# First attention of a four-layer kernel: one exp of half the scores, scaled and squared, in place of two exps with a shift between

## The chip, the cores and the metric

The kernel runs on one core of a Trainium2 chip. The metric is the device time of one execution in microseconds; times inside the profiled execution are counted from its first instruction.

## The reference

The whole kernel computes four layers over x of shape (32, 16, 16, 64): a shifted-window attention, a convolution with computed taps (involution), a linear attention with a mixture of experts, and a second linear attention with a routed mixture. The change touches the first:

```
xw  = windows of the rolled, group-normed x        # 128 windows of 64 tokens, 8 heads of 8
attn = (qn @ kn^T) * scale + bias + mask           # qn, kn: rows of length 1
attn = softmax(attn)
out  = attn @ v, then @ Wo.T + bo, rolled back, and added to x
```

A softmax may be taken of shifted scores, since the quotient stays the same: exp(s - c) / sum exp(s - c).

## The kernel before

**Tiling.** The activations lie channel by token: 128 partitions (64 channels of two halves of the batch) by 4096 columns, eight chunks of 512 (`NCH`). The attention works in 64 window pairs (`PAIRS`), two to a unit: 32 units (`UNITS`), four to a chunk (`PER`). A unit has two halves b = 2u and 2u+1, each a tile of 128 by 512 scores in a PSUM bank of its own (banks 0 to 3 in turns of two units).

**A unit before.** POOL spreads the unit's queries over the heads (`stage_queries`, L692). PE writes bias and mask (L1939, two matmuls) and then the products of queries and keys (L1945, 16 small matmuls) into the two banks. ACT takes exp of half the scores of each bank into a bf16 tile (`exp_half`, L1576). PE sums these over the keys with a matrix of ones into bank 4 (`sum_halves`, L1955), so that every row holds the sum. DVE reads the sum's bits as an integer, which is nearly its logarithm, and makes of it the level to take away, minus twice that logarithm (L914), and adds the level to the scores (L919), both in `shift_down`. ACT takes exp of the shifted scores (`exp_scores`, L1584). PE multiplies with the values (L1966) and sums for the denominator (L1969), both in `weigh`, into bank 5 or 6. ACT inverts the denominator by Ln and Exp (`invert_sums`, L1590 and L1592), DVE multiplies (`divide_unit`, L924). Once per chunk PE projects (`project_out`, L1981), DVE adds the result to the image in nine pieces (`add_images`, L934) and takes the statistics of the next norm (`image_stats`, L309 and L313), and ACT adds a bias to the image (`add_bias`, L1595).

**Order.** Each engine has its own list, written out by hand as a loop over k, and the engines meet at counted semaphores: `when("l0_summed", n)` is the wait until step l0_summed has been done n times. In iteration k PE does the first sum of unit k-1, the scores of unit k, the second sum of unit k-1, the weighing of unit k-2 and, in one of four, a projection. The scores of unit k wait until both halves of unit k-2 are shifted:

```
            def scores(u):
                pe.wait_ge(*when("l0_staged", u + 1))
                if u >= 2:
                    pe.wait_ge(*when("l0_shifted", 2 * (u - 1)))
```

There is one sum bank, so a sum waits until DVE has read the one before. ACT alternates the exp of half the scores of unit k with the exp of the shifted scores of unit k-1.

Elsewhere in the kernel stand L1027 (a product of two SBUF tiles on DVE), L741, L713, L750 and L767 (subtractions and a product on POOL) and L1216 (a cast on DVE), which are quoted below.

Of the kernel before, what the change touches and what calls it, by code (L numbers as in the profile page):

```python
# [5 lines left out]
F32, F16, BF16 = mybir.dt.float32, mybir.dt.float16, mybir.dt.bfloat16  # L6
# [21 lines left out]
LEVEL = -2.0 * float(np.log(2.0)) / 2.0 ** 23, 254.0 * float(np.log(2.0))  # L28
# [118 lines left out]
def network(nc, xw_d, xi_d, mats_d, vecs_d, feats_d, cw1_d, wmask_d, taps_d, wexp_d, wo0_d,  # L147
            w1l2_d, w2l2_d, w1l3_d, w3l3_d, w2l3_d, out_d, slots_d, results_d):
    with ExitStack() as ctx:
# [98 lines left out]
        SC = [stage[:, 1024 + s * 512:1536 + s * 512] for s in range(2)]  # L248
        PX = [stage[:, 2048 + s * 512:2560 + s * 512] for s in range(4)]
# [6 lines left out]
        EH = [spare[:, 512 + 256 * s:768 + 256 * s].bitcast(BF16) for s in range(2)]  # L256
        LV = [spare[:, 1024 + 512 * s:1536 + 512 * s] for s in range(2)]
# [50 lines left out]
        def gn_image(dve, t, src, b):  # L308
            nc.vector.bn_stats(stats[:, b, :], src[:, b, :]).then_inc(S(t + "_stats"), 1)  # L309
# [331 lines left out]
        def _(pool):  # L641
# [56 lines left out]
            pool.wait_ge(*when("hmask", 2))  # L698
            for u in range(UNITS):
                stage_queries(u)  # L700
# [135 lines left out]
        def _(dve):  # L836
# [74 lines left out]
            def shift_down(b):  # L911
                u, g = b // 2, b % 2
                dve.wait_ge(*when("l0_summed", b + 1))
                nc.vector.tensor_scalar(LV[b % 2], bank[4][:, :].bitcast(I32), LEVEL[0], LEVEL[1],  # L914
                                        ALU.mult, ALU.add).then_inc(S("l0_level"), 1)
                dve.wait_ge(*when("l0_level", b + 1))
                if b >= 2:
                    dve.wait_ge(*when("l0_exp", b - 1))
                nc.vector.tensor_tensor(SC[b % 2], bank[2 * (u % 2) + g][:, :], LV[b % 2], ALU.add) \  # L919
                    .then_inc(S("l0_shifted"), 1)  # L920

            def divide_unit(u):
                dve.wait_ge(*when("l0_rsum", u + 1))
# [3 lines left out]
            def add_images(c):  # L927
                dve.wait_ge(*when("xi_biased", c + 1))
                dve.wait_ge(*when("l0_wo", c + 1))
                yw = bank[7][:, :].rearrange("p (b w i j) -> p b w i j", w=NWIN, i=WS, j=WS)  # L930
                for wy, iy, r, nr in runs:
                    for wx, ix, q, nq in runs:
                        xv = Xi[:, 2 * c:2 * c + 2, r:r + nr, q:q + nq]
                        nc.vector.tensor_tensor(xv, xv, yw[:, :, 2 * wy + wx, iy:iy + nr, ix:ix + nq], ALU.add)                             .then_inc(S("x1_ready"), 1)  # L934

            def image_stats(c):
                dve.wait_ge(*when("x1_ready", 9 * (c + 1)))
                for b in (2 * c, 2 * c + 1):
                    gn_image(dve, "g1", X3, b)
                for b in (2 * c, 2 * c + 1):  # L940
                    gn_total(dve, "g1", b)
# [4 lines left out]
            for k in range(1, UNITS + PER + 1):  # L946
                if k <= UNITS:
                    shift_down(2 * k - 2)
                if 3 <= k < UNITS + 3:
                    divide_unit(k - 3)  # L950
                if k <= UNITS:
                    shift_down(2 * k - 1)
                if k % PER == 3 and k >= 7:
                    add_images(k // PER - 1)
                if k % PER == 0 and k >= 8:
                    image_stats(k // PER - 2)
# [589 lines left out]
        def _(act):  # L1546
# [24 lines left out]
            def exp_half(b):  # L1571
                u, g = b // 2, b % 2
                act.wait_ge(*when("l0_scores", u + 1))
                if b >= 2:
                    act.wait_ge(*when("l0_summed", b - 1))
                nc.scalar.activation(EH[b % 2], bank[2 * (u % 2) + g][:, :], ACT.Exp, scale=0.5) \  # L1576
                    .then_inc(S("l0_half"), 1)

            def exp_scores(b):
                u = b // 2  # L1580
                act.wait_ge(*when("l0_shifted", b + 1))
                if u >= 2:
                    act.wait_ge(*when("l0_pv", u - 1))
                nc.scalar.activation(PX[b % 4], SC[b % 2], ACT.Exp).then_inc(S("l0_exp"), 1)  # L1584

            def invert_sums(u):
                act.wait_ge(*when("l0_pv", u + 1))
                if u >= 2:
                    act.wait_ge(*when("l0_out", u - 1))
                nc.scalar.activation(RS[u % 2], bank[5 + u % 2][:, 256:512], ACT.Ln).then_inc(S("l0_lnsum"), 1)  # L1590
                act.wait_ge(*when("l0_lnsum", u + 1))
                nc.scalar.activation(RS[u % 2], RS[u % 2], ACT.Exp, scale=-1.0).then_inc(S("l0_rsum"), 1)  # L1592
# [13 lines left out]
            for k in range(UNITS + 2):  # L1606
                for g in range(2):
                    if k < UNITS:
                        exp_half(2 * k + g)
                    if 1 <= k <= UNITS:  # L1610
                        exp_scores(2 * k - 2 + g)
                if k >= 2:
                    invert_sums(k - 2)
                if k % PER == 1 and k < UNITS:
                    add_bias(k // PER)
# [264 lines left out]
        def _(pe):  # L1880
# [52 lines left out]
            def scores(u):  # L1933
                pe.wait_ge(*when("l0_staged", u + 1))
                if u >= 2:
                    pe.wait_ge(*when("l0_shifted", 2 * (u - 1)))
# [14 lines left out]
            def sum_halves(b):  # L1951
                pe.wait_ge(*when("l0_half", b + 1))
                if b >= 1:
                    pe.wait_ge(*when("l0_level", b))
                nc.tensor.matmul(bank[4][:, :], sum16, EH[b % 2], start=True, stop=True).then_inc(S("l0_summed"), 1)  # L1955

            def weigh(u):
# [4 lines left out]
                parts = [PX[(2 * u + g // 2) % 4].rearrange("p (j x n) -> p j x n", j=2, x=2)[:, :, g % 2, :]  # L1962
# [723 lines left out]
```

## Time and profile before

| what | value |
|---|---|
| time, three runs | median 1014.98 us (1014.89 to 1015.75) |
| profiled execution | 1015.97 us |
| its span, first to last instruction | 1014.0 us |
| mean granted TensorE clock | 0.938 of full |
| first attention, first scores to last addition | about 72 to 217 us |
| busy over the span | PE 84%, DVE 82%, ACT 69%, POOL 60% |

PE is TensorE, DVE VectorE, ACT ScalarE, POOL GpSimd, PEld TensorE's weight load. A duration is that of the instruction as recorded; instructions of one engine overlap a little, so the work of an engine is better read from the distance between two starts. The idle time behind a row in brackets is that ahead of the instruction, with the line that ended it.

### The profile page before, as it was taken

The numbers are of one execution on the slowest core, as the hardware profiler recorded it, in microseconds if no ns is written. First come the engines' busy times: TensorE is split into PE (matmuls) and PEld (weight loads), VectorE is DVE, ScalarE is ACT, GpSimd is POOL, SyncE is SP. The second block draws the span as 40 slices with busy tenths as digits, with TensorE's granted clock in tenths as the row PEclk, the third lists the DMA queues.
The fourth block names the chain that finished last, engine by engine and source line by source line (L and its number), as shares of the span: only waits on it lengthen the run. The fifth ranks groups of instructions, "written<-read, shape, count | busy, mean of one in ns | idle before, by whom it ended". The sixth has DMA issues, their size and how long they took to land.

```text
span 1014.0 us, 20687 instructions
## 1 busy us (share of the span) xinstructions
PE 855.2 (84%) x6419; PEld 478.1 (47%) x6440; DVE 830.1 (82%) x1720; ACT 697.0 (69%) x1318; POOL 604.0 (60%) x645
## 2 busy tenths in 40 slices
PE   4958888859999998788888987589999999999960
PEld 3433333424445763344355544255555556555640
DVE  7987888878866856687768888589999999999986
ACT  1867777736447556555777664288889999999966
POOL 1952222214787654277504777777777788888880
PEclk9978999979999999599999999599999999999985
DMA  6000000020003210000300000211111111111107
GB/s 246 1 2 2 2 2 2 2 79 0 1 1 114 70 44 0 1 2 1 100 1 14 27 26 26 61 56 47 39 45 41 33 34 35 33 35 36 36 21 250
DMA packets 25807, 39.64 MB, mean 39 GB/s; under 512 B 6436, under 2 KB 14632, under 8 KB 25448
## 3 DMA queue, kind: packets, MB, share of 16 engines
q1 hardware_dynamic: 16616, 28.93, 9.0%
q0 software_dynamic: 9088, 9.39, 2.8%
q8 instruction: 58, 0.95, 0.4%
q14 instruction: 45, 0.37, 0.1%
HBM read 24.83 MB, written 13.47 MB: 38 GB/s over the span
## 4 chain that ended last, share of the span: by engine, by line
PE 43%; DVE 23%; POOL 15%; issue 9%; ACT 7%; DMA 1%; POOLq 0%; SPq 0%; another core or an unknown queue 0%; ACTq 0%; DVEq 0%
PE bank L2495 9%; POOL results L808 6%; PE bank L2468 5%; POOL slots L785 4%; PE bank L2028 3%; DVE KSS L914 3%; POOL stage L767 3%; DVE stage L919 2%; PE bank L1945 2%; PE bank L1981 2%; DVE T L896 2%; PE bank L2045 1%; PE bank L2257 1%; PE bank L2070 1%; PE bank L1939 1%
## 5 line engine op out<-in xcount | busy, mean ns | idle before, releaser
L2495 PE MATMUL bank<-stage,big 128*128 128x512 f16 (+1 forms) x858 | 226.4, 384 | 6.9 <-issue 3.0
L808 POOL DMA_INDIRECT results<-T,small x156 | 177.7, 1139 | 44.3 <-issue 35.6
L785 POOL DMA_INDIRECT slots<-T,index x128 | 127.1, 993 | 79.3 <-DVE index L1347 41.4
L1855 ACT ACTIVATE T<-bank 128x512 f32<-128x512 f32 x234 | 139.5, 596 | 28.8 <-PE bank L2495 21.8
L1837 ACT ACTIVATE stage<-T 128x512 f16<-128x512 f32 x234 | 146.4, 626 | 3.5 <-DVE T L1494 2.1
L1494 DVE TENSOR_TENSOR T<-bank,T 128x512 f32<-128x512 f32 x195 | 133.8, 686 | 12.3 <-ACT T L1855 8.3
L1517 DVE TENSOR_TENSOR T<-T,stage 128x512 f16<-128x512 f32 x170 | 117.4, 690 | 1.2
L2495 PEld LDWEIGHTS bank<-stage,big 128*128 (+1 forms) x858 | 78.1, 101 | 59.1 <-issue 17.2
L692 POOL TENSOR_TENSOR stage<-T,small 128x512 f32<-128x512 f32 x32 | 34.2, 1068 | 99.0 <-PE bank L1945 99.0
L2468 PE MATMUL bank<-l2w,stage 128*128 (+1 forms) x936 | 90.8, 219 | 0.1
L2468 PEld LDWEIGHTS bank<-l2w,T 128*128 128x128 f16 x780 | 53.7, 98 | 69.3 <-issue 46.4
L2468 PE MATMUL bank<-l2w,T 128*128 x780 | 76.2, 220 | 9.4 <-DVE T L1517 4.9
L2468 PEld LDWEIGHTS bank<-l2w,stage 128*128 128x128 f16 (+1 forms) x936 | 63.9, 98 | 9.3 <-issue 1.3
L713 POOL TENSOR_TENSOR stage<-stage 128x512 f16<-128x512 f32 x40 | 46.1, 1160 | 33.6 <-ACT stage L1636 32.6
L914 DVE TENSOR_SCALAR KSS<-bank 128x512 f32<-128x512 int32 x64 | 43.7, 683 | 23.1 <-PE bank L1955 14.6
L767 POOL TENSOR_TENSOR stage<-stage 128x256 f16<-128x256 f32 x64 | 43.4, 695 | 30.4 <-DVE stage L1216 30.0
L1576 ACT ACTIVATE KSS<-bank 128x512 bf16<-128x512 f32 x64 | 37.6, 589 | 30.0 <-PE bank L1945 30.0
L989 DVE TENSOR_TENSOR stage<-bank,big 128x512 f32<-128x512 f32 x72 | 46.9, 687 | 8.7 <-PE bank L2045 6.4
L1700 ACT ACTIVATE stage<-bank,small 128x256 f32<-128x256 f32 x64 | 30.2, 474 | 27.5 <-PE bank L2223 27.0
L1636 ACT ACTIVATE stage<-stage 128x512 f16<-128x512 f32 x40 | 25.2, 630 | 33.6 <-DVE stage L989 33.6
L2257 PE MATMUL bank<-T,mats 128*128 128x512 f32 x64 | 37.0, 666 | 12.8 <-ACT T L1720 12.1
L1584 ACT ACTIVATE stage<-stage 128x512 f32<-128x512 f32 x64 | 40.1, 626 | 10.9 <-DVE stage L919 8.6
(395 smaller groups left out, 1970.9 us busy)
## 6 DMA issues: line engine op xcount, KB each, us to landing
stage<-slots SPq DMA_DIRECT2D x39, 130.0 KB, 2.1
stage<-in_w3l SPq DMA_DIRECT2D x8, 373.0 KB, 3.0
stage<-in_w1l SPq DMA_DIRECT2D x8, 320.0 KB, 3.0
results<-T,small POOLq DMA_INDIRECT x156
T<-in_xw SPq DMA_DIRECT2D x4, 512.0 KB, 6.1
X<-in_xi SPq DMA_DIRECT2D x1, 2048.0 KB, 13.4
slots<-T,index POOLq DMA_INDIRECT x128, 2.2
X<-results SPq DMA_DIRECT2D x8, 256.0 KB, 5.5
```

What stands on the lines that cost most here:

```text
L767: nc.gpsimd.tensor_tensor(HID_LO[n % 4], HID[n % 4], HID_HI[n % 4], ALU.subtract).then_inc(S("low3"), 1)
L785: pool.indirect_dma_start(slots_d, bass.IndirectOffsetOnAxis(ap=index[:, k, n:n + 1], axis=0), rows5[:, n * RW:(n + 1) * RW], None).then_i ...
L808: pool.indirect_dma_start(results_d, bass.IndirectOffsetOnAxis(ap=IDS[t % 4][:, i:i + 1], axis=0), Y5[t % 2][:, i, :], None).then_inc(S(f" ...
L914: nc.vector.tensor_scalar(LV[b % 2], bank[4][:, :].bitcast(I32), LEVEL[0], LEVEL[1], ALU.mult, ALU.add).then_inc(S("l0_level"), 1)
L989: nc.vector.tensor_tensor(product(k).rearrange("p (b r c) -> p b r c", r=HH, c=WW), bank[k % 6][:, :].rearrange("p (b r c) -> p b r c", r= ...
L1494: nc.vector.tensor_tensor(H5[q], bank[3 + q][:, :], S5[q], ALU.mult).then_inc(S("hid5"), 1)
L1517: nc.vector.tensor_tensor(LO5[q], H5[q], HI5[q], ALU.subtract).then_inc(S("low5"), 1)
L1837: nc.scalar.activation(HI5[q][r], H5[q][r], ACT.Copy).then_inc(S("high5"), 1)
L1855: nc.scalar.activation(S5[q][to], bank[q][r, :], ACT.Silu).then_inc(S("silu5"), 1)
L2257: nc.tensor.matmul(out, mat("mean"), T2P[c], start=True, stop=True).then_inc(S4(op), 1)
L2468: mm = nc.tensor.matmul(bank[6 + s][:, i * 128:(i + 1) * 128], H[:, i * 128:(i + 1) * 128], downs[rows_down, bass.ds(w, 2 * C)], start=(k ...
L2495: mm = nc.tensor.matmul(to[0:m, :], big16[:, bass.ds(e * UPW + o, m)], XT[s], start=(v % 2 == 0), stop=(v % 2 == 1))
```

## The change

The second exp is gone. The exp of half the scores, now kept in f32, is multiplied by the inverse of its sum and then squared, which gives the exp of the shifted scores: (exp(s/2) / sum)^2. The inverse is again made from the bits of the sum: `INVERSE` minus the integer, read as a float, is nearly the reciprocal (`invert_level`). Of a unit's two halves DVE multiplies the first (`scale_down`), POOL the second; ACT squares both (`square`). The exps of half the scores are written to eight tiles in turn (`EX`, `HELD`), in which all the rest is done in place; the sum matmul reads the high 16 bits of each f32 element as bf16, every second 16-bit element of the tile. The order changes too: ACT does the inversion of the denominators, both exps of unit k, then both squares of unit k-2; DVE does both inversions ahead of the division; POOL stages two units ahead; weighing comes one iteration later and the projection, the additions and the statistics later and in smaller parts.

```
@@ POOL
             pool.wait_ge(*when("hmask", 2))
+            stage_queries(0)
+            stage_queries(1)
             for u in range(UNITS):
-                stage_queries(u)
+                if u + 2 < UNITS:
+                    stage_queries(u + 2)
+                b = 2 * u + 1
+                pool.wait_ge(*when("l0_inverse", b + 1))
+                nc.gpsimd.tensor_tensor(EX[b % HELD], EX[b % HELD], RV[1], ALU.mult) \
+                    .then_inc(S("l0_scaled_pool"), 1)
@@ DVE
-            def shift_down(b):
-                u, g = b // 2, b % 2
+            def invert_level(b):
                 dve.wait_ge(*when("l0_summed", b + 1))
-                nc.vector.tensor_scalar(LV[b % 2], bank[4][:, :].bitcast(I32), LEVEL[0], LEVEL[1],
-                                        ALU.mult, ALU.add).then_inc(S("l0_level"), 1)
-                dve.wait_ge(*when("l0_level", b + 1))
-                if b >= 2:
-                    dve.wait_ge(*when("l0_exp", b - 1))
-                nc.vector.tensor_tensor(SC[b % 2], bank[2 * (u % 2) + g][:, :], LV[b % 2], ALU.add) \
-                    .then_inc(S("l0_shifted"), 1)
+                if b % 2 and b >= 3:
+                    dve.wait_ge(*when("l0_scaled_pool", b // 2))
+                nc.vector.tensor_scalar(RV[b % 2].bitcast(I32), bank[4][:, :].bitcast(I32), -1.0, INVERSE,
+                                        ALU.mult, ALU.add).then_inc(S("l0_inverse"), 1)
+
+            def scale_down(b):
+                dve.wait_ge(*when("l0_inverse", b + 1))
+                nc.vector.tensor_tensor(EX[b % HELD], EX[b % HELD], RV[0], ALU.mult).then_inc(S("l0_scaled"), 1)
...
-            for k in range(1, UNITS + PER + 1):
+            for k in range(1, UNITS + 2 * PER + 1):
                 if k <= UNITS:
-                    shift_down(2 * k - 2)
-                if 3 <= k < UNITS + 3:
-                    divide_unit(k - 3)
-                if k <= UNITS:
-                    shift_down(2 * k - 1)
-                if k % PER == 3 and k >= 7:
-                    add_images(k // PER - 1)
-                if k % PER == 0 and k >= 8:
-                    image_stats(k // PER - 2)
+                    invert_level(2 * k - 2)
+                    scale_down(2 * k - 2)
+                    invert_level(2 * k - 1)
+                if 4 <= k < UNITS + 4:
+                    divide_unit(k - 4)
+                c = k // PER - 2
+                if k % PER == 1 and c >= 0:
+                    add_images(c, 0)
+                if k % PER == 2 and c >= 0:
+                    add_images(c, 1)
+                if k % PER == 3 and c >= 0:
+                    image_stats(c, 0)
+                    image_stats(c, 1)
+                if k % PER == 0 and c >= 1:
+                    image_totals(c - 1)
@@ ACT
             def exp_half(b):
                 u, g = b // 2, b % 2
                 act.wait_ge(*when("l0_scores", u + 1))
-                if b >= 2:
-                    act.wait_ge(*when("l0_summed", b - 1))
-                nc.scalar.activation(EH[b % 2], bank[2 * (u % 2) + g][:, :], ACT.Exp, scale=0.5) \
+                if u >= 4:
+                    act.wait_ge(*when("l0_pv", u - 3))
+                nc.scalar.activation(EX[b % HELD], bank[2 * (u % 2) + g][:, :], ACT.Exp, scale=0.5) \
                     .then_inc(S("l0_half"), 1)
 
-            def exp_scores(b):
...
+            def square(b):
+                act.wait_ge(*when("l0_scaled_pool" if b % 2 else "l0_scaled", b // 2 + 1))
+                nc.scalar.activation(EX[b % HELD], EX[b % HELD], ACT.Square).then_inc(S("l0_exp"), 1)
...
-            for k in range(UNITS + 2):
-                for g in range(2):
-                    if k < UNITS:
-                        exp_half(2 * k + g)
-                    if 1 <= k <= UNITS:
-                        exp_scores(2 * k - 2 + g)
-                if k >= 2:
-                    invert_sums(k - 2)
+            for k in range(UNITS + 4):
+                if k >= 4:
+                    invert_sums(k - 4)
+                if k < UNITS:
+                    exp_half(2 * k)
+                    exp_half(2 * k + 1)
+                if 2 <= k < UNITS + 2:
+                    square(2 * k - 4)
+                    square(2 * k - 3)
                 if k % PER == 1 and k < UNITS:
                     add_bias(k // PER)
@@ PE
             def scores(u):
                 pe.wait_ge(*when("l0_staged", u + 1))
                 if u >= 2:
-                    pe.wait_ge(*when("l0_shifted", 2 * (u - 1)))
+                    pe.wait_ge(*when("l0_half", 2 * (u - 1)))
...
             def sum_halves(b):
                 pe.wait_ge(*when("l0_half", b + 1))
                 if b >= 1:
-                    pe.wait_ge(*when("l0_level", b))
-                nc.tensor.matmul(bank[4][:, :], sum16, EH[b % 2], start=True, stop=True).then_inc(S("l0_summed"), 1)
+                    pe.wait_ge(*when("l0_inverse", b))
+                high = EX[b % HELD].bitcast(BF16).rearrange("p (n v) -> p n v", v=2)[:, :, 1]
+                nc.tensor.matmul(bank[4][:, :], sum16, high, start=True, stop=True).then_inc(S("l0_summed"), 1)
...
-            for k in range(UNITS + 3):
+            for k in range(UNITS + 5):
...
-                if 2 <= k < UNITS + 2:
-                    weigh(k - 2)
-                if k % PER == 2 and k >= 6:
-                    project_out(k // PER - 1)
+                if 3 <= k < UNITS + 3:
+                    weigh(k - 3)
+                if k % PER == 0 and k >= 8:
+                    project_out(k // PER - 2)
```

## Rows read from the trace of the kernel before

**Rows 1.** The page's first line.
```profile
span 1014.0 us, 20687 instructions
```

**Rows 2.** Stretches: us, each engine's busy us (instructions), granted clock, DMA.
```profile
72.00:82.00 10.00, 7.78 (x43) 2.93 (x45) 3.17 (x6) 2.94 (x6) 2.08 (x2) 0.50 0.00 0
...
98.40:114.80 16.40, 14.27 (x186) 6.48 (x184) 14.00 (x34) 12.32 (x26) 4.17 (x4) 1.00 0.01 1
```

**Rows 3.** Waits from 98.4 to 196.6 us: total us, times, longest.
```profile
PE bank L1939 <- DVE stage L919: 8.8, 18, 1.0
...
ACT KSS L1576 <- PE bank L1945: 16.2, 18, 1.8
```

**Rows 4.** PE's timeline in one chunk: start, us, line, operands, count.
```profile
147.16 1.09 PE L1945 MATMUL bank<-stage,T 32*64 32x256 f32 x16
148.18 0.39 PE L1955 MATMUL bank<-KSS,rows 128*128 128x512 bf16 x1
148.50 0.64 PE L1966 MATMUL bank<-stage,big 128*32 128x128 f32 x16
148.96 0.61 PE L1969 MATMUL bank<-stage,small 128*32 128x256 f32 x8
149.51 1.98 PE L1981 MATMUL bank<-T,big 128*128 128x512 f32 x4
151.33 0.38 PE L1955 MATMUL bank<-KSS,rows 128*128 128x512 bf16 x1
151.54 0.59 PE L1939 MATMUL bank<-big,rows 128*128 128x512 f16 x2
152.07 1.09 PE L1945 MATMUL bank<-stage,T 32*64 32x256 f32 x16
```

**Rows 5.** PE's timeline at the attention's start, middle and end.
```profile
81.86 1.01 PE L1939 MATMUL bank<-big,rows 128*128 128x512 f16 x2
...
86.92 0.59 PE L1939 MATMUL bank<-big,rows 128*128 128x512 f16 x2 [0.52 <-DVE stage L919]
...
105.98 0.59 PE L1939 MATMUL bank<-big,rows 128*128 128x512 f16 x2 [0.27 <-DVE stage L919]
...
203.52 0.39 PE L1955 MATMUL bank<-KSS,rows 128*128 128x512 bf16 x1
...
212.18 1.22 PE L1981 MATMUL bank<-T,big 128*128 128x512 f32 x1 [1.41 <-DVE T L924]
```

**Rows 6.** POOL's L750 and L713: ns min/median/max, first and last start, shapes.
```profile
L750 POOL TENSOR_TENSOR T<-T x8: 1035/1040/1477, 322.4 to 360.1; 128x512 f32<-128x512 f32 x8
...
L713 POOL TENSOR_TENSOR stage<-stage x40: 1155/1160/1163, 239.2 to 297.0; 128x512 f16<-128x512 f32 x40
```

**Rows 7.** Timeline of POOL and DVE, later in the kernel.
```profile
327.94 1.40 POOL L741 TENSOR_TENSOR big<-stage,big 128x640 f16<-128x640 f32 x1
328.25 1.63 DVE L1027 TENSOR_TENSOR T<-T 128x512 f32<-128x512 f32 x1
...
334.72 0.69 DVE L1027 TENSOR_TENSOR T<-T 128x512 f32<-128x512 f32 x1 [0.42 <-ACT T L1645]
```

**Rows 8.** DVE's timeline in the chunk of rows 4.
```profile
151.74 0.69 DVE L914 TENSOR_SCALAR KSS<-bank 128x512 f32<-128x512 int32 x1 [1.72 <-PE bank L1955]
152.47 0.69 DVE L919 TENSOR_TENSOR stage<-bank,KSS 128x512 f32<-128x512 f32 x1
153.08 0.41 DVE L924 TENSOR_TENSOR T<-bank,KSS 128x256 f32<-128x256 f32 x1
```

**Rows 9.** Timeline: an instruction on DVE and what it releases, twice.
```profile
161.45 0.68 DVE L914 TENSOR_SCALAR KSS<-bank 128x512 f32<-128x512 int32 x1
...
162.28 0.38 PE L1955 MATMUL bank<-KSS,rows 128*128 128x512 bf16 x1 [0.16 <-DVE KSS L914]
...
428.55 0.29 DVE L1216 CAST stage<-stage 128x256 f16<-128x256 f32 x1 [0.78 <-ACT stage L1700]
428.92 0.67 POOL L767 TENSOR_TENSOR stage<-stage 128x256 f16<-128x256 f32 x1 [0.40 <-DVE stage L1216]
```

More of the change, by code:

```diff
@@ L3 @@
 from contextlib import ExitStack
+import itertools
 import numpy as np
@@ L27 @@
 PER = UNITS // NCH
-LEVEL = -2.0 * float(np.log(2.0)) / 2.0 ** 23, 254.0 * float(np.log(2.0))
+INVERSE = 254.0 * 2.0 ** 23
+HELD = 8
 RR, KK, PH = 16, 9, HH + 2
@@ L247, in network @@
         QX = [stage[:, s * 512:(s + 1) * 512] for s in range(2)]
-        SC = [stage[:, 1024 + s * 512:1536 + s * 512] for s in range(2)]
-        PX = [stage[:, 2048 + s * 512:2560 + s * 512] for s in range(4)]
         PROD = [stage[:, s * 512:(s + 1) * 512] for s in range(6)]
@@ L255, in network @@
         RS = [spare[:, 256 * s:256 * s + 256] for s in range(2)]
-        EH = [spare[:, 512 + 256 * s:768 + 256 * s].bitcast(BF16) for s in range(2)]
-        LV = [spare[:, 1024 + 512 * s:1536 + 512 * s] for s in range(2)]
+        RV = [spare[:, 512 + 512 * s:1024 + 512 * s] for s in range(2)]
+        EX = [stage[:, 1024 + 512 * s:1536 + 512 * s] for s in range(HELD - 1)] + [spare[:, 1536:2048]]
         both16 = rows[:, 0, 0:64].bitcast(F16)
@@ L922, in divide_unit, with add_images @@
+            def scale_down(b):
+                dve.wait_ge(*when("l0_inverse", b + 1))
+                nc.vector.tensor_tensor(EX[b % HELD], EX[b % HELD], RV[0], ALU.mult).then_inc(S("l0_scaled"), 1)
             def divide_unit(u):
-                dve.wait_ge(*when("l0_rsum", u + 1))
+                dve.wait_ge(*when("l0_rsum", 2 * u + 2))
                 nc.vector.tensor_tensor(T34[:, 256 * u:256 * u + 256], bank[5 + u % 2][:, 0:256], RS[u % 2],
                                         ALU.mult).then_inc(S("l0_out"), 1)
-            def add_images(c):
-                dve.wait_ge(*when("xi_biased", c + 1))
-                dve.wait_ge(*when("l0_wo", c + 1))
+            def add_images(c, part):
+                if part == 0:
+                    dve.wait_ge(*when("xi_biased", c + 1))
+                    dve.wait_ge(*when("l0_wo", c + 1))
@@ L930, in add_images @@
                 yw = bank[7][:, :].rearrange("p (b w i j) -> p b w i j", w=NWIN, i=WS, j=WS)
-                for wy, iy, r, nr in runs:
-                    for wx, ix, q, nq in runs:
+                for i, ((wy, iy, r, nr), (wx, ix, q, nq)) in enumerate(itertools.product(runs, runs)):
+                    if (i >= 4) == part:
                         xv = Xi[:, 2 * c:2 * c + 2, r:r + nr, q:q + nq]
-                        nc.vector.tensor_tensor(xv, xv, yw[:, :, 2 * wy + wx, iy:iy + nr, ix:ix + nq], ALU.add)                             .then_inc(S("x1_ready"), 1)
@@ L936, in image_stats, with image_totals @@
-            def image_stats(c):
+                        nc.vector.tensor_tensor(xv, xv, yw[:, :, 2 * wy + wx, iy:iy + nr, ix:ix + nq], ALU.add) \
+                            .then_inc(S("x1_ready"), 1)
+            def image_stats(c, b):
                 dve.wait_ge(*when("x1_ready", 9 * (c + 1)))
-                for b in (2 * c, 2 * c + 1):
-                    gn_image(dve, "g1", X3, b)
+                gn_image(dve, "g1", X3, 2 * c + b)
+            def image_totals(c):
                 for b in (2 * c, 2 * c + 1):
@@ L1573, in exp_half @@
                 act.wait_ge(*when("l0_scores", u + 1))
-                if b >= 2:
-                    act.wait_ge(*when("l0_summed", b - 1))
-                nc.scalar.activation(EH[b % 2], bank[2 * (u % 2) + g][:, :], ACT.Exp, scale=0.5) \
+                if u >= 4:
+                    act.wait_ge(*when("l0_pv", u - 3))
+                nc.scalar.activation(EX[b % HELD], bank[2 * (u % 2) + g][:, :], ACT.Exp, scale=0.5) \
                     .then_inc(S("l0_half"), 1)
-            def exp_scores(b):
[L1580 to L1584, printed above, removed]
+            def square(b):
+                act.wait_ge(*when("l0_scaled_pool" if b % 2 else "l0_scaled", b // 2 + 1))
+                nc.scalar.activation(EX[b % HELD], EX[b % HELD], ACT.Square).then_inc(S("l0_exp"), 1)
             def invert_sums(u):
@@ L1589, in invert_sums @@
                     act.wait_ge(*when("l0_out", u - 1))
-                nc.scalar.activation(RS[u % 2], bank[5 + u % 2][:, 256:512], ACT.Ln).then_inc(S("l0_lnsum"), 1)
-                act.wait_ge(*when("l0_lnsum", u + 1))
+                nc.scalar.activation(RS[u % 2], bank[5 + u % 2][:, 256:512], ACT.Ln).then_inc(S("l0_rsum"), 1)
+                act.wait_ge(*when("l0_rsum", 2 * u + 1))
                 nc.scalar.activation(RS[u % 2], RS[u % 2], ACT.Exp, scale=-1.0).then_inc(S("l0_rsum"), 1)
@@ L1961, in weigh @@
                 to = bank[5 + u % 2]
-                parts = [PX[(2 * u + g // 2) % 4].rearrange("p (j x n) -> p j x n", j=2, x=2)[:, :, g % 2, :]
+                parts = [EX[(2 * u + g // 2) % HELD].rearrange("p (j x n) -> p j x n", j=2, x=2)[:, :, g % 2, :]
                          for g in range(HP)]
```

## The prediction

> **What bounds the kernel now.** The page comes first: the span is 1014.0 us [rows 1], inside a profiled execution of 1015.97 us; the median of the plain runs is 1014.98 us. The change touches the first attention alone, so the question is what sets the pace there. The table of stretches gives it by chunk of four units (a unit is two window pairs, eight chunks in all): 16.40 us hold PE 14.27, DVE 14.00, ACT 12.32 and POOL 4.17 us of busy time at the full granted clock [rows 2]. Nothing is full, and PE and DVE are close to it. The waits say which engine makes which wait: PE's bias matmul of the next scores waited 8.8 us in six chunks for DVE's shift (L919), ACT's first exponential waited 16.2 us for PE's scores [rows 3]. This is a ring: scores of unit k wait until DVE has shifted both halves of unit k-2, since the shift reads the scores' own bank; the shift waits for the sum matmul, that for ACT, that for scores. The chain of waits in one chunk goes through the same places and is led by L914 and L919.
>
> PE's own work without waits is read from the distance between starts in PE's timeline [rows 4]: sum matmul to bias matmuls 151.33 to 151.54, 0.21 us; bias matmuls to query matmuls 0.53; query matmuls to the next sum 147.16 to 148.18, 1.02; that sum to weighing 0.32; L1966 to L1969 0.46; L1969 to what follows 0.55. A unit is 3.09 us, called 3.1, and a projection (149.51 to 151.33) adds 1.82. Four units and a projection make 14.2 us. Before, the bias matmuls of unit 3 start at 86.92, of unit 8 at 105.98, and the sum matmul that stands where a unit 32 would start is at 203.52 [rows 5], so its bias matmuls would be at 203.73: 97.75 us for six chunks, 16.3 each.
>
> **The change, part by part.** *Removed from DVE:* all 64 shifts L919 of 0.69 us. L914 stays, with other constants and an int32 output: same bank, same 512 columns, 0.69 us taken. *Added to DVE:* 32 multiplications of two SBUF tiles, 0.69 us when alone (L1027 at 334.72) [rows 7]. DVE falls from 14.0 to about 14.0 - 4 x 0.69 = 11.2 us per chunk. *ACT:* the exp of a bank stays, with an f32 output in place of a bf16 one; the second exp becomes a square of the same 512 columns from SBUF to SBUF. I price both as what they replace and keep the 12.3 us of the chunk [rows 2]. Both exps now go first and wait for scores alone. ACT's 12.3 us stay below PE's 14.2. *POOL:* 32 multiplications of two full f32 tiles. The nearest row, L750, has a median of 1.04 us, and I take it; L713, a subtraction with f16 operands, has 1.16 us, the upper end [rows 6]. POOL's work doubles from 4.17 to 8.3 us per chunk, far from full, but it stands beside DVE at the wrong time, see below. *PE:* scores now wait for the two exps of unit k-2 and no longer for DVE; this takes the ring apart. The weighing and the projection come one and two iterations later; their buffers (eight tiles, the two PSUM banks of outputs) are freed in time: the output's division in DVE iteration k-1 is wanted by the weighing at PE iteration k, the squares of unit k-3 end in ACT iteration k-1. I cost them at nothing in steady state. If this cover goes, PE waits at L1957.
>
> *The new ring.* PE's one sum bank is left: a sum waits until DVE has inverted the sum before. Let S be the start of a unit's first sum matmul. DVE starts the first inversion 0.41 us later (151.33 to 151.74) and the next dependent operation 0.73 us after that (151.74 to 152.47) [rows 4, 8]: the multiplication wants to begin at S+1.14. PE issues the second sum at S+1.76, so the second inversion can begin at S+2.18 and the next S comes from PE at S+3.1. DVE alone is ready: 1.14+0.61 is 1.75.
>
> *The shared port.* Rows 7 show what happens when DVE reads two SBUF tiles while POOL reads SBUF. L1027 took 1.63 us instead of 0.69: it was dispatched at 328.25, POOL's L741 ran from 327.94 to 329.34, and DVE ended 0.54 us after that. In the other direction the longest L750 took 1.48 us instead of 1.04 [rows 6]; it is the one that began at 329.31, while that L1027 was still running. So whichever is second waits for the first to end. Now the order of POOL: multiplication of unit k's second half after the second inversion (0.08 us after its end, as from 428.84 to 428.92 [rows 9]), then at once the staging L692, 1.04 us each. With the next S at 0.83 us after the start of that inversion (161.45 to 162.28 [rows 9]), POOL's pair runs from S-0.05 to S+2.09, with 0.06 us between. DVE's multiplication at S+1.14 finds the staging (begun at S+1.05) on the port, ends at 2.09+0.54, and the second inversion begins at S+2.55 instead of S+2.18. The unit is then 2.55+0.83 = 3.38 us instead of 3.10. The additions to the image and the statistics lie before that wait and are covered by it, so I cost them at nothing; without the wait DVE's slack in a unit is 2.18 - 1.75 = 0.4 us, and what they have beyond it would be PE's wait.
>
> The unit with a projection lasts 3.10+1.82 = 4.92 us and lets POOL finish before S: the next unit is free of the wait, 3.10. In the one after it POOL's pair ends at S+2.00, 3.29 us; then 3.38. A chunk is 4.92+3.10+3.29+3.38 = 14.69 us (the projection's unit takes the wait in its slack).
>
> The Trainium skill, SBUF — State Buffer, section Who interferes with whom, speaks against this change: a DVE instruction with two SBUF inputs contends with a GpSimd instruction that reads SBUF, and the loser blocks fully. The trace agrees, with the 1.63 us above; by the rule the chunk is the 14.69 us, and without it PE's 14.2.
>
> *The strided operand.* The sum matmul now reads every second 16-bit element of a 32-bit tile. No row has that; the lower bound is 0.21 us of issue as now, the upper one is taken from a real 32-bit operand, L1981, four in 1.82 us, 0.455 each [rows 4]. I take 0.21, since type and columns don't change and only the distance of the elements does. The Trainium skill, SBUF — State Buffer, section Door 1: The DMA port swizzle, says that at least two accesses per 16-byte line keep full speed; that stride has four. No run here shows it, and the sum by it is the one I took.
>
> *Start and end.* The units 0 to 2 run with the granted clock at 0.50 [rows 2]. There the scores of unit 2 need no longer wait for the shift (81.86 in the trace [rows 5]), and the weighing of unit 0 moves out of unit 2: scores of unit 3 at about 86.3, 0.6 us earlier. But PE has less to do in that stretch, so the clock may rise one unit later: a unit of 5.06 us at half clock (81.86 to 86.92) instead of 3.38 costs 1.7 us. Taken: 0.6 of the range 0 to 1.7. At the end the projection at 212.18 comes 8.66 us after the sum at 203.52 [rows 5]. With the new order I count: sum at 0, second inversion 1.8 to 2.5, POOL 3.6, squares after the inverse sums of unit 29 to 5.1, weighing of unit 31 from 5.4 to 6.4, its inverse sums 7.8, division 8.2, projection 8.4. That is 0.2 us less. POOL's multiplication (1.04 instead of 0.69) is in it.
>
> **The sum.** Scores of unit 8: 86.3 + 5 x 3.38 = 103.2. Place of unit 32: 103.2 + 6 x 14.69 = 191.3, against 203.73: 12.4 us. End 0.2 more, clock 0.6 less: 12.0 us. The span becomes 1002.0 us, and the median 1014.98 - 12.0 = 1003.0 us. What follows the attention is taken to move as it is; the loads released at its end (the taps) keep their distance to the last weighing.
>
> **Rivals.**
> A, the port costs nothing (0.15). The tie at S+1.05 against S+1.14 is 0.09 us; if DVE is first, POOL's staging is late, and it has more than 1 us to spare. Then the unit is PE's 3.1: 86.3 + 15.5 + 6 x 14.2 = 187.0, a gain of 16.7, with the end's 0.2 and the clock's 0.6 about 16 us: 999 us.
> B, the strided operand streams at half rate (0.12), 0.42 us per sum matmul. For it: the 512 columns lie over twice the bytes. The unit becomes 3.10+0.42 = 3.52 and the chunk 15.9 us: unit 32 at 86.3+17.6+95.4 = 199.3, a gain of 4.4, with end and clock 4.0: 1011 us.
> C, the division or the squares come late (0.08), so that PE waits at the weighing: 0.2 to 0.5 us per unit on top, 6 to 16 us back in all; 1009 us with 0.2, 1015 with 0.4. Against it: ACT reaches the squares about a microsecond after they are due from POOL.
> D, slower (0.07). The strided operand is read at the pace of the 32-bit one or worse. With y for a sum matmul the chunk is 14.2 + 8 (y - 0.21), and it equals the 16.4 of before at y = 0.48; four times the present price (0.85) gives 19.3 us per chunk, 24 us more: 1039 us. Against it: four times the price for a distance of two elements would be out of proportion, though no row excludes it.
> My forecast has 0.58.
>
> **How the numbers follow.** 0.2% is 2 us, about what a measurement of this kernel can tell from no change. Slower is D with a small part of C: 0.07. No change is what B and C leave near 1015: 0.04. Faster: 0.89. The range has A at its low end (PE's work alone, 998) and B at its high end with a microsecond of C: 998 to 1012; C's upper part and D are outside.
>
> **What would show it.** In the profile after: L919's successor gone from DVE, 32 multiplications there, those beside POOL's staging at 1.2 to 1.5 us and the others at 0.69; units of 3.3 to 3.4 us beside ones of 3.1, 14.7 us per chunk; PE's remaining waits on the inversion and not on scores' release; ACT's first exp still waiting for scores; POOL's multiplication at 1.04 to 1.2 us; the sum matmul at 0.38 us. The prediction is wrong if the sum matmul lasts over 0.4 us, if PE waits at the weighing, or if the granted clock stays low beyond unit 3.

## The result, and the profile after

The changed kernel takes 1000.33 us (median of four, 999.29 to 1002.24), the one before 1014.93 us on the same chip: 14.6 us less, a ratio of 0.9869 (95% interval 0.9846 to 0.9893, that is 10.9 to 15.6 us). Forecast were 12.0 us less and 1003.0 us, in a range from 998 to 1012.

The page of the changed kernel has a span 16.5 us shorter than in [rows 1]; the row below it is 24 of POOL's 32 new multiplications (count, busy us, mean ns; the other 8 are a group of the same length).

```profile
span 997.5 us, 20590 instructions
...
L706 POOL TENSOR_TENSOR stage<-stage,KSS 128x512 f32<-128x512 f32 x24 | 30.6, 1277 | 35.1 <-DVE KSS L922 35.1
```

The stretches of the attention after, against the second of [rows 2]: POOL is busy for 10.4 us of 16.3 in place of 4.2 of 16.4. A chunk is now shorter than this stretch, so the row holds some work of the next one. The first row is the start, where [rows 2] had a granted clock of 0.50.

```profile
80.00:84.00 4.00, 2.46 (x22) 1.15 (x23) 2.60 (x4) 2.44 (x5) 3.16 (x3) 0.98 0.00 0
...
114.80:131.10 16.30, 14.92 (x188) 7.21 (x195) 14.29 (x33) 13.03 (x29) 10.37 (x10) 1.00 0.01 2
```

One chunk in the timeline of the changed kernel: PE's bias matmuls of five units (L1953), which answer to L1939 in [rows 4, 5]. Two of the sum matmuls ahead of them (L1970) are shown with their wait.

```profile
120.06 0.59 PE L1953 MATMUL bank<-big,rows 128*128 128x512 f16 x2
...
123.18 0.59 PE L1953 MATMUL bank<-big,rows 128*128 128x512 f16 x2 [0.17 <-issue]
...
126.38 0.39 PE L1970 MATMUL bank<-stage,rows 128*128 128x512 bf16 x1 [0.25 <-DVE KSS L922]
126.61 0.59 PE L1953 MATMUL bank<-big,rows 128*128 128x512 f16 x2
...
129.89 0.39 PE L1970 MATMUL bank<-stage,rows 128*128 128x512 bf16 x1 [0.33 <-DVE KSS L922]
130.12 0.59 PE L1953 MATMUL bank<-big,rows 128*128 128x512 f16 x2
...
135.04 0.59 PE L1953 MATMUL bank<-big,rows 128*128 128x512 f16 x2
```

The distances are 3.12, 3.43, 3.51 and 4.92 us: 14.98 us per chunk (forecast 14.69; before 16.37). The two longer units end in a wait of the sum matmul for DVE's inversion. Why that is late stands in the rows of DVE and POOL in the second of these four units. Its first sum matmul starts at S = 122.95, 0.23 us ahead of the bias matmuls:

```profile
123.57 0.69 DVE L922 TENSOR_SCALAR KSS<-bank 128x512 int32<-128x512 int32 x1
124.29 1.35 DVE L927 TENSOR_TENSOR stage<-stage,KSS 128x512 f32<-128x512 f32 x1
125.56 0.68 DVE L922 TENSOR_SCALAR KSS<-bank 128x512 int32<-128x512 int32 x1
...
122.81 1.28 POOL L706 TENSOR_TENSOR stage<-stage,KSS 128x512 f32<-128x512 f32 x1 [2.20 <-DVE KSS L922]
124.04 1.04 POOL L692 TENSOR_TENSOR stage<-T,small 128x512 f32<-128x512 f32 x1
```

DVE's multiplication was dispatched at 124.29, 0.25 us after POOL's staging had begun. The staging ends at 125.08 and DVE 0.56 us later, so it took 1.35 us, and the second inversion began at S+2.61 in place of S+2.21. This is the meeting of [rows 7], where the forecast had put it. In the units ahead of the first projection the two arrive 20 to 60 ns apart, and who is first changes from unit to unit:

```profile
87.92 1.03 POOL L692 TENSOR_TENSOR stage<-T,small 128x512 f32<-128x512 f32 x1
87.98 1.52 DVE L927 TENSOR_TENSOR stage<-stage,KSS 128x512 f32<-128x512 f32 x1
...
91.40 0.69 DVE L927 TENSOR_TENSOR stage<-stage,KSS 128x512 f32<-128x512 f32 x1
91.42 1.57 POOL L692 TENSOR_TENSOR stage<-T,small 128x512 f32<-128x512 f32 x1
```

When POOL is second nobody waits for it, and the unit is PE's 3.12 us; when DVE is second it is 3.42 to 3.43 us. After such a longer unit POOL comes later in the next, and DVE is first by 20 ns.

In the chunks with a projection DVE is second in every unit but the one behind the projection. The rows of the third unit (S = 126.38) show what has changed:

```profile
126.49 0.60 DVE L942 TENSOR_TENSOR X<-X,bank 128x32 f32<-128x32 f32 x5
127.00 0.68 DVE L922 TENSOR_SCALAR KSS<-bank 128x512 int32<-128x512 int32 x1
127.72 1.42 DVE L927 TENSOR_TENSOR stage<-stage,KSS 128x512 f32<-128x512 f32 x1
...
127.55 1.04 POOL L692 TENSOR_TENSOR stage<-T,small 128x512 f32<-128x512 f32 x1
```

POOL's staging begins at S+1.17, as in the unit at 91.42, where DVE was ready at S+1.15 and came first. Here five additions stand ahead of DVE's first inversion, and its multiplication is ready only at S+1.34.

### The profile page after: what moved, and what is told of

It is laid out like the page before. It is cut to its first block, busy times and chain, and to the rows that moved or that the text cites. A ratio compares the mean times of both kernels' runs of the same rounds, so it can differ in the third digit from the quotient of the medians.

```text
span 997.5 us, 20590 instructions
## 1 busy us (share of the span) xinstructions
PE 847.7 (85%) x6419; PEld 477.8 (48%) x6440; DVE 820.7 (82%) x1688; ACT 692.7 (69%) x1318; POOL 645.0 (65%) x677
## 4 chain that ended last, share of the span: by engine, by line
PE 42%; DVE 19%; POOL 18%; issue 11%; ACT 8%; DMA 1%; POOLq 0%; another core or an unknown queue 0%; SPq 0%; ACTq 0%; DVEq 0%
PE bank L2510 10%; POOL slots L792 7%; POOL results L815 7%; PE bank L2483 6%; PE bank L2043 3%; POOL stage L774 3%; DVE KSS L922 2%; PE bank L1959 2%; PE bank L1996 2%; DVE T L903 1%; PE bank L2060 1%; ACT X L1890 1%; PE bank L2272 1%; PE bank L1970 1%; POOL T L827 1%
## 5 line engine op out<-in xcount | busy, mean ns | idle before, releaser
L1510 DVE TENSOR_TENSOR T<-bank,T 128x512 f32<-128x512 f32 x195 | 134.1, 688 | 12.6 <-ACT T L1869 8.4
L922 DVE TENSOR_SCALAR KSS<-bank 128x512 int32<-128x512 int32 x64 | 43.8, 684 | 21.4 <-PE bank L1970 13.6
L706 POOL TENSOR_TENSOR stage<-stage,KSS 128x512 f32<-128x512 f32 x24 | 30.6, 1277 | 35.1 <-DVE KSS L922 35.1
L1592 ACT ACTIVATE stage<-bank 128x512 f32<-128x512 f32 x56 | 30.7, 594 | 29.5 <-PE bank L1959 29.5
L692 POOL TENSOR_TENSOR stage<-T,small 128x512 f32<-128x512 f32 x32 | 36.2, 1133 | 11.0 <-PE bank L1959 11.0
```

The lines of the kernel that those rows point to most:

```text
L922: nc.vector.tensor_scalar(RV[b % 2].bitcast(I32), bank[4][:, :].bitcast(I32), -1.0, INVERSE, ALU.mult, ALU.add).then_inc(S("l0_inverse"), 1)
L1510: nc.vector.tensor_tensor(H5[q], bank[3 + q][:, :], S5[q], ALU.mult).then_inc(S("hid5"), 1)
```

## The experiments

All twelve, with the distances between PE's unit starts at steady clock (the unit behind a projection first; the last holds the projection) and the ratio to the kernel before, measured beside it on the same chip. e0, e1, e2 and e3 ran on one chip, e4 (the kernel before again), e5, e6 and e7 on a second, e8 to e11 on a third. Most of the differences are better read from the chunk than from the time, which moves with the granted clock as well.

| run | units, us | chunk, us | median, us | ratio (95%) |
|---|---|---|---|---|
| before again (e4) | 3.55, 4.09, 3.83, 4.91 | 16.38 | 1014.71 (one) | |
| changed, again (e0) | 3.13, 3.42, 3.52, 4.93 | 15.00 | 996.80 | 0.9853 (0.9793 to 0.9914) |
| changed, again (e7) | 3.12, 3.43, 3.51, 4.93 | 14.99 | 999.57 | 0.9871 (0.9844 to 0.9897) |
| e1, multiplication last | 3.13, 3.38, 3.31, 5.26 | 15.08 | 999.84 | 0.9886 (0.9836 to 0.9936) |
| e2, DVE multiplies both | 3.13, 4.35, 4.35, 5.46 | 17.29 | 1012.19 | 1.0002 (0.9981 to 1.0024) |
| e3, as e2, with the old wait | 3.55, 3.69, 3.63, 4.96 | 15.83 | 1007.18 | 0.9951 (0.9923 to 0.9980) |
| e6, as e2, without staging | 3.12, 3.51, 3.51, 5.45 | 15.59 | 1006.40 | 0.9925 (0.9901 to 0.9950) |
| e5, additions between | 3.12, 3.12, 3.13, 4.93 | 14.30 | 993.59 | 0.9810 (0.9780 to 0.9840) |
| e5 again (e11) | 3.13, 3.12, 3.13, 4.93 | 14.31 | 997.17 | 0.9830 (0.9791 to 0.9869) |
| e8, as e5, DVE multiplies both | 3.13, 3.50, 3.39, 5.20 | 15.22 | 1002.63 | 0.9897 (0.9862 to 0.9932) |
| e9, changed, with the old wait | 4.13, 4.13, 4.12, 4.93 | 17.31 | 1021.65 | 1.0081 (1.0053 to 1.0110) |
| e10, ACT alternates | 3.12, 3.43, 3.51, 4.92 | 14.98 | 1000.08 | 0.9859 (0.9815 to 0.9904) |

**The changed kernel and the one before, again.**

> The changed kernel once more, unaltered, for a second profile and as the base of the others. If the earlier rise of the granted clock at the attention's start (unit 3 at 83.9 us instead of the 86.3 forecast) belongs to the change, it is there again, with unit 8 near 100 us; if it was an accident of one execution, unit 3 starts at 86 to 87 us and the span is 2 to 3 us longer than 997.5. Chunks of 14.98 us in both cases.

> The changed kernel unaltered, as the base on this chip for the next run: chunk 14.98 us, time 995 to 1001 us. Its third profile also tells how far the start of unit 3 moves with the granted clock from one execution to the next (83.9 and 81.5 us so far).

> The kernel before once more, for its profile. If the start of unit 3 is set by the change (86.9 us before, 83.9 and 81.5 after), it is again at 86 to 87 us, with the granted clock at 0.50 until 84 us. If the clock moves by itself from one execution to the next, it may be anywhere between 83 and 87. The chunk stays at 16.37 us; the last projection took 3.45 us at half clock and 1.98 us after the change, and shows the same question at the end.

Unit 3 of the changed kernel started at 83.94, 81.47 and 86.34 us in three executions, that of the kernel before at 86.92 and 86.53. The granted clock, from 80 to 84 us in the second and in the third execution of the changed kernel:

```profile
80.00:84.00 4.00, 2.86 (x44) 1.55 (x45) 2.66 (x5) 2.97 (x6) 3.75 (x3) 1.00 0.02 4
```
```profile
80.00:84.00 4.00, 3.12 (x16) 1.15 (x19) 2.68 (x3) 1.69 (x3) 2.27 (x2) 0.50 0.00 0
```

The same program gets 2.4 GHz or 1.2 GHz there, and up to 4.9 us hang on it. It isn't the change that sets it in a given execution; whether it makes the early rise more frequent, two profiles of the kernel before don't tell. The times of the kernel before move too: 50 executions on the three chips of the experiments took 1007.8 to 1019.3 us, one of 1007.83 with a mean granted clock of 0.949 and the one of 1019.25 with 0.935. At the end it is steadier: the last projection took 1.98 us in all three of the changed kernel and 3.45 and 3.78 us in the two before. Against the kernel before on the same chip the change was worth 14.6, 16.3 and 14.5 us.

**e1: the multiplication behind both inversions.**

```
                     invert_level(2 * k - 2)
-                    scale_down(2 * k - 2)
                     invert_level(2 * k - 1)
+                    scale_down(2 * k - 2)
```

(In e1, e5 and e11 the first inversion also waits for DVE's own multiplication before it, which reads the same tile. That multiplication stands earlier in DVE's own list, so the wait is met by then.)

> DVE does both inversions of a unit first and its multiplication after them. Theory: DVE's multiplication waits for POOL's staging (1.3 to 1.4 us instead of 0.69) and holds back the second inversion and with it PE's next sum. Then the units of 3.43 and 3.51 us become 3.1 to 3.15, the chunk falls from 14.98 to 14.2 to 14.4 us, and the time by 4 to 5 us against the changed kernel. Rival: PE's waits at the sum come from the inversion's own latency or from ACT; then the order on DVE changes nothing and the chunk stays at 15.0 us.

The expectation failed in the sum and held in its first half. The units without additions became 3.12 us, all of them, and DVE's multiplication 0.68 us. But the chunk stayed, and the time was no lower (999.84 us against 996.80 for the changed kernel on this chip). Now the statistics (0.74 us) and additions stand between the multiplication and the next first inversion, which starts at 112.65 where its sum matmul was issued at 111.35:

```profile
111.06 0.68 DVE L929 TENSOR_TENSOR stage<-stage,KSS 128x512 f32<-128x512 f32 x1
111.66 0.42 DVE L933 TENSOR_TENSOR T<-bank,KSS 128x256 f32<-128x256 f32 x1
111.99 0.74 DVE L309 BATCH_NORM_STATS2 small<-X 128x6 f32<-128x256 f32 x2
112.65 0.67 DVE L924 TENSOR_SCALAR KSS<-bank 128x512 int32<-128x512 int32 x1
113.90 0.69 DVE L924 TENSOR_SCALAR KSS<-bank 128x512 int32<-128x512 int32 x1 [0.57 <-remote]
```

DVE then idles 0.57 us behind it, waiting for the second sum. The wait at the port had been covering the additions. In the unit with the projection the late inversion makes PE wait too: 5.26 us in place of 4.93.

**e5: the additions into that idle time.**

```
             if k <= UNITS:
                 invert_level(2 * k - 2)
+            (additions or statistics of this iteration)
+            if k <= UNITS:
+                invert_level(2 * k - 1)
                 scale_down(2 * k - 2)
-                invert_level(2 * k - 1)
             if 4 <= k < UNITS + 4:
                 divide_unit(k - 4)
-            (additions or statistics of this iteration)
```

> DVE's order in an iteration: first inversion, additions or statistics, second inversion, multiplication, division. With the multiplication moved last alone, units without additions fell to 3.12 us but the additions then delayed the first inversion, and the chunk stayed at 15.07. Theory: both delays together make the chunk's 0.7 us over PE's work; with the additions in DVE's idle time between the two inversions the chunk is 14.2 to 14.4 us and the time 4 to 5 us below the changed kernel in the same call. Rival: POOL, whose multiplication now waits for DVE (1.65 us), or ACT is next in line within 0.3 us; then the chunk is 14.8 us or more.

> The version with the additions between the two inversions once more, as the base of this call: chunk 14.30 us, time 991 to 997 us.

The chunk is 14.30 us, PE's own work; from 94 to 180 us no matmul waits for another engine. The time is 6.0 us below the changed kernel on the same chip (993.59 against 999.57), of which 6 x 0.69 = 4.1 us are the chunks and about 0.6 the five units ahead of the first projection; the rest is within what the start's clock moves. In e11 the chunk was the same, but the time of 997.17 us lay just above the 991 to 997 expected, 2.9 us below e10 (1000.08), which has the changed kernel's chunk. So the chunk repeats, and the gain in time is about 3 to 6 us. POOL's multiplication is now second at the port in every unit and takes 1.65 us, and that costs nothing:

```profile
113.88 1.65 POOL L706 TENSOR_TENSOR stage<-stage,KSS 128x512 f32<-128x512 f32 x1 [0.47 <-DVE KSS L924]
115.50 1.03 POOL L692 TENSOR_TENSOR stage<-T,small 128x512 f32<-128x512 f32 x1
```

**e9: the old wait put back.**

```
                 if u >= 2:
+                    pe.wait_ge(*when("l0_scaled_pool", u - 1))
                     pe.wait_ge(*when("l0_half", 2 * (u - 1)))
```

> The changed kernel, in which the scores of unit k wait again until both halves of unit k-2 have been multiplied (POOL's comes last), as they waited for the shifts before. Theory: the release of the scores is what pays: from the start of the second inversion 0.69 + 0.08 + 1.27 us of POOL, 0.15 to the scores, 1.55 us of scores and 0.4 us to the next second inversion make a unit of 4.1 to 4.2 us, the chunk is 17.0 to 17.6 us and the time 13 to 18 us above the changed kernel. Rival: the scores are ready in time anyway; then the chunk stays at 15.0 us.

Units of 4.13 us and a chunk of 17.31 us, as worked out; slower than the kernel before. The time is 21 us above the changed kernel's (21.6 above e10 on the same chip), above the 13 to 18 expected. The chunks make 14.0 of it, and the five units ahead of the first projection pay 0.9 us each as well (4.13 against 3.24 on average), together 18.4; the rest is not accounted for. The added wait is for POOL's multiplication of 1.28 us, where the old one was for DVE's shift of 0.69, so e9 shows what such a wait costs in this kernel and not what the old one cost.

**e2, e3, e6: DVE multiplies both halves.** In e2 DVE's order is inversion, multiplication, inversion, multiplication:

```
                     invert_level(2 * k - 1)
+                    scale_down(2 * k - 1)
```

and POOL's multiplication goes. e3 has in addition `pe.wait_ge(*when("l0_scaled", 2 * (u - 1)))` ahead of the scores, in place of the wait for the exps; e6 is e2 without 30 of the 32 stagings on POOL.

> DVE multiplies both halves (order: inversion, multiplication, inversion, multiplication), POOL only stages. Theory: PE's release from the shift is what pays, and POOL's share pays little, since DVE gets 4 x 0.69 us per chunk more (14.0 in all) but no longer waits for the port as often. Unit by distances on DVE 3.0 plus 0.5 for additions and statistics: chunk 14.6 to 15.4 us, time within 3 us of the changed kernel. Rival: the work taken off DVE is what pays; then the chunk goes back to about 16 us and the time to 1008 to 1012 us.

> As the run in which DVE multiplies both halves, and in addition the scores of unit k wait until DVE has multiplied both halves of unit k-2, as they waited for the shifts in the kernel before. Theory: this ring set the pace before, so its return alone costs what the change brought: chunk 16.2 to 16.6 us, time 1010 to 1015 us, 8 to 12 us above the run without the wait. Rival: DVE's amount of work sets the pace; then the wait costs under 2 us beside the run without it.

> As the run in which DVE multiplies both halves, but POOL stages only the queries of units 0 and 1 and leaves out the other 30 stagings; the scores are taken from those two tiles, all else is done in full. Theory: the units of 4.35 us in that run come from DVE's first multiplication (1.54 us) meeting POOL's staging on the port; without the staging it is 0.69 us everywhere and the units are 3.1 to 3.6 us, the chunk 14.5 to 15.3 us instead of 17.28, the time 10 to 16 us lower. Rival: the amount of work on DVE, with the additions, makes them; then the chunk stays above 16.5 us.

All three expectations failed in their numbers. e2 was no faster than the kernel before, e3, with the later wait, was 5 us faster than e2, and e6 was in ratio about 8 us faster than e2, not 10 to 16. The lengths of DVE's multiplications (nanoseconds: least, median, greatest) tell why, in e2, in e3 and in e6:

```profile
L921 DVE TENSOR_TENSOR stage<-stage,KSS x56: 691/693/1544, 77.7 to 205.2; 128x512 f32<-128x512 f32 x56
```
```profile
L921 DVE TENSOR_TENSOR stage<-stage,KSS x56: 691/693/814, 77.0 to 199.9; 128x512 f32<-128x512 f32 x56
```
```profile
L918 DVE TENSOR_TENSOR stage<-stage,KSS x56: 691/692/693, 76.7 to 195.7; 128x512 f32<-128x512 f32 x56
```

In e2 the additions delay the first inversion so that the multiplication behind it meets the staging, 40 ns apart (111.61 and 111.65), and takes 1.54 us. In e3 the scores come later, the staging waits for them, and the two overlap only at their edge (0.81 us at most). In e6 there is nothing to meet, and the chunk is 1.7 us shorter than in e2. It isn't the 14.5 to 15.3 us expected. The rest is put down to DVE's work in the units with additions, which lie ahead of the first inversion; e8 moves them and is still at 15.22.

**e8: the same in the good order.** As e5, with both multiplications on DVE behind the second inversion.

> DVE multiplies both halves, in the better order: first inversion, additions, second inversion, both multiplications, division; POOL only stages. Theory: DVE's distances sum to 13.3 to 13.6 us per chunk, under PE's 14.3, and what made DVE alone slow (17.28 us per chunk) was the meeting with the staging ahead of the second inversion and the additions ahead of the first. Then POOL's share of the multiplications is worth little once the order is right: chunk 14.3 to 15.0 us, time within 4 us of the base of this call. Rival: without POOL's share DVE is the bound in any order; then the chunk is above 15.5 us, and the time 9 us or more above the base.

15.22 us per chunk, between the two expectations, and in time 5.5 us above e11. DVE hardly meets the staging (its multiplications take 0.79 us at most). Its distances in a unit with additions are about 0.6 for each of two inversions, the additions and two multiplications, and 0.33 for the division: 3.4 us, over PE's 3.1. The idle time in the projection's unit isn't there for the others. So in this order POOL's share is worth 0.9 us per chunk (15.22 against 14.31).

**e10: ACT alternates.**

> The changed kernel with ACT's order as it was in kind before: one exp, one square, the other exp, the other square. Theory: ACT has 0.4 to 2 us of idle time per unit ahead of the first exp and what it makes is wanted later, so the order of exps and squares is worth nothing: chunk 14.98 to 15.1 us, time 996 to 1001 us. Rival: the second sum matmul waits for the second exp; then every unit grows by up to 0.5 us and the time by 6 to 16 us.

No difference, in chunk or time: the new order on ACT is worth nothing by itself.

## Why the prediction was right, point by point

**The scores' release pays.** Right: e9 puts a wait of that kind back and the chunk goes from 14.98 to 17.31 us. It isn't enough by itself: e2 has the release and gains nothing. How the 1.4 us per chunk divide between the release and the work taken off DVE the runs don't show, since in e2 and e3 the meeting with the staging changes along with the wait.

**The meeting at the port.** Right in place, direction and result: [rows 7] gave an end 0.54 us after POOL's, measured was 0.56. The forecast units were 3.10, 3.29, 3.38 and 4.92 us, measured 3.12, 3.43, 3.51 and 4.92. e1 and e5 take the meeting away. The Trainium skill, SBUF — State Buffer, section Who interferes with whom, states this lock; the trace agrees in both directions: 1.52 us for DVE as the second, 1.57 for POOL.

**A term off: POOL's multiplication**, 1.28 us in place of 1.04. I took L750 [rows 6], which multiplies a tile by itself. The trace had a nearer row, L669, an addition of two different f32 tiles with a median of 1.28 us:

```profile
L669 POOL TENSOR_TENSOR T<-T,big x4: 1272/1282/1597, 45.9 to 56.0; 128x512 f32<-128x512 f32 x4
```

The pair of POOL therefore began 1.23 us apart and not 1.10: 0.13 us in each of the two longer units, 1.6 us in six chunks. The prediction's own sign for this multiplication, 1.04 to 1.2 us, was missed.

**A term off the other way: the first units.** All were to be 3.38 us; they alternate between 3.12 and 3.42, since the tie of rival A (0.09 us by my sum) fell both ways. The longer multiplication of POOL is behind this too: after a longer unit it puts the staging at S+1.17, behind DVE's S+1.15, where the forecast had it at S+1.05. From the start of unit 3 to that of unit 8 it took 16.2 us in place of 16.9. Rival A came true in every second unit there, and nowhere later.

**The additions at nothing.** Right only in part. Where DVE is second in any case they are covered by the wait. But in the third unit of a chunk (127.00 to 127.72 above) they are what makes DVE second: without them the tie would fall as at 91.40, and the unit would be 3.12 us in place of 3.51. By these rows they cost about 0.4 us per chunk, an estimate, since no run moves them alone in the changed kernel. e1 shows the other case: without the port's wait they cost 0.8 us per chunk (15.08 against 14.30 in e5).

**The strided operand.** Rival B and D are out: from the sum to the bias matmuls are 0.23 us (119.83 to 120.06) against 0.21 before, and the sum's duration is 0.40 against 0.39, just at the 0.4 us that the prediction named as its sign of being wrong. The price of rival D at its worst is 3 to 4 us too high by its own terms (five units of 4.38 and six chunks of 19.3 us come to about 20 us more, not 24). The Trainium skill's rule, SBUF — State Buffer, section Door 1: The DMA port swizzle, has full speed at this stride; the runs agree but for those 0.02 us.

**Rival C** is out: in the changed kernel's waits from 90 to 180 us the matmuls wait for nothing but the inversion (2.3 and 2.0 us) and PE's own issue.

**Start and end.** Where the clock rose late (e7) unit 3 came at 86.34 us, as forecast (86.3); in the execution profiled first it rose early and gave 2.4 us more. The last projection of e7 is at 199.98, 12.2 us ahead of 212.18 [rows 5]; the forecast had 12.6 without the clock. What I missed is its duration. Before, PE was idle 1.57 us ahead of the last weighing and 1.41 us ahead of the projection, and its granted clock was 0.50 from 208.8 to 212.2 us. After, the pause ahead of the weighing is gone, and the clock stays at 1.00 in all three profiles. The first two rows are of the kernel before, the third is the stretch of the last projection in the first profile after:

```profile
208.80:212.20 3.40, 1.95 (x25) 1.00 (x25) 1.05 (x4) 1.48 (x4) 1.31 (x2) 0.50 0.15 24
212.18 3.45 PE L1981 MATMUL bank<-T,big 128*128 128x512 f32 x4 [1.41 <-DVE T L924]
...
197.50:199.60 2.10, 1.98 (x4) 0.68 (x4) 0.86 (x4) 0.00 (x0) 0.04 (x1) 1.00 0.87 340
```

That is another 1.5 us. That the missing pause is what keeps the clock up is likely and was not tried. Of the 1.5 us, 0.8 are lost again in a longer pause ahead of the next layer's first small matmul (3.98 us in e7, 3.21 before). Like for like, e7 against the kernel before, the first matmul of the next layer starts at 208.64 in place of 221.54, 12.9 us earlier, and the span is 13.1 us shorter. The forecast of 12.0 is inside the interval of 10.9 to 15.6; the measured 14.6 compares executions in which the clock rose at different moments. Term by term (rounded), e7 against the kernel before:

| term, us gained | forecast | measured |
|---|---|---|
| up to the start of unit 3 | 0.6 | 0.6 |
| from there to unit 8 | 2.2 | 2.8 |
| six chunks | 9.6 | 8.2 |
| last sum to last projection | 0.2 | 0.5 |
| last projection's duration | nothing | 1.5 |
| pause behind it | nothing | -0.8 |
| clock at the start | -0.6 | (in the first row) |
| sum | 12.0 | 12.9 |

The mechanism was right. That the sum came within 1 us is in part luck: the chunks gave 1.4 us less than forecast, and the first units and the end made up for it.

## What to carry to other kernels

Where DVE multiplies two SBUF tiles and POOL reads SBUF, look at who arrives second: give the wait to the engine whose result is wanted later, by order and not by chance, and then look at what the wait had been covering. Put small work into the idle time between two dependent instructions of a loop, not at its end. An engine's sum over four units says nothing when one of them has the slack and the others don't; count unit by unit.

## What the runs showed of the hardware

A POOL product of two different f32 tiles of 128 by 512 took 1.28 us (L706), one of a tile with itself (L750) or of two broadcast operands (L692) 1.04 us. DVE's multiplication took 0.69 us where it was ready 20 ns ahead of POOL's staging (91.40), and 1.52 us where it was 60 ns behind it (87.98). With an unchanged program the granted clock at the attention's start rose to stay at 1.00 at about 72 us in e0, 80 us in the execution profiled first, and after 84 us in e7. In the execution profiled first, DVE's two small operations ahead of the next norm took 0.49 and 1.05 us in place of the 0.17 and 0.18 of the kernel before. Each ended within 0.05 us of the end of one of POOL's two casts (203.52 and 204.62):

```profile
202.38 1.14 POOL L715 CAST big<-big 128x1152 f16<-128x1152 f32 x1 [4.85 <-DMA big<-in_wexp]
203.07 0.49 DVE L324 TENSOR_TENSOR small<-small 128x16 f32<-128x16 f32 x1
203.47 1.15 POOL L716 CAST big<-big 128x1152 f16<-128x1152 f32 x1
203.59 1.05 DVE L326 TENSOR_TENSOR small<-small 128x16 f32<-128x16 f32 x1
```

The attention's end had come nearer to the arrival of what the casts read. It looks like the same meeting; no run tried it.
